# Mixture-of-experts kernel: routing ahead of the weight splits, and a first expert loop that waits for its weights expert by expert

## The reference

```python
def ffn(x):                                    # 8 experts, 2 chosen
    logits = x @ W_gate + b_gate               # W_gate [512, 8]
    _, top_idx = top_k(logits, 2)
    y_all = relu(einsum('bsd,edh->bseh', x, W_e) + b_e)   # W_e [8, 512, 512]
    return take_along_axis(y_all, top_idx[..., None], 2).mean(2)

x = x + 0.5 * ffn(layernorm(x))
x = x + attention(layernorm(x))                # one head, width 128
x = x + 0.5 * ffn(layernorm(x))                # the same weights again
```

## Time and profile before

| | us |
|---|---|
| median of 3 runs | 309.33 (308.43 to 310.49) |
| span of the profiled execution | 309.0 |
| PE busy | 258.0 (84%) |
| DVE busy | 180.9 (59%) |
| POOL busy | 147.6 (48%) |
| ACT busy | 98.5 (32%) |

### The profile page before, as it was taken

How to read it: one execution, slowest core, us unless ns; L and a number is a source line. 1 busy time by engine, 2 the same in 40 slices (tenths; PEclk the granted TensorE clock), 3 DMA queues, 4 the chain that set the end, 5 groups by cost and what they waited for, 6 DMA issues and landing times. The chain is left out here.

```text
span 309.0 us, 4801 instructions
## 1 busy us (share of the span) xinstructions
PE 258.0 (84%) x1271; PEld 184.7 (60%) x1272; DVE 180.9 (59%) x379; ACT 98.5 (32%) x177; POOL 147.6 (48%) x150
## 2 busy tenths in 40 slices
PE   7948674899999999994999998838999999999400
PEld 2314222378888888853878684413888888888300
DVE  4995989733444434367688837884344344443691
ACT  0652642324233342411234533221232433324100
POOL 4570653735666656334856400005356666563450
PEclk9975855799999999997999999996999999999955
DMA  6995641384453434526230101213354444345792
GB/s 243 378 405 200 225 137 48 97 267 158 158 169 126 148 127 161 178 68 185 78 136 0 70 15 55 83 55 97 105 147 151 167 132 159 116 159 200 286 319 108
DMA packets 22434, 47.24 MB, mean 153 GB/s; under 512 B 4237, under 2 KB 4877, under 8 KB 22417
## 3 DMA queue, kind: packets, MB, share of 16 engines
q1 hardware_dynamic: 12208, 22.35, 20.9%
q0 software_dynamic: 7360, 20.46, 20.8%
q10 hardware_dynamic: 2850, 4.23, 3.7%
HBM read 32.34 MB, written 18.35 MB: 164 GB/s over the span
## 5 line engine op out<-in xcount | busy, mean ns | idle before, releaser
L442 POOL DMA_INDIRECT z_dram<-yrow,place x46 | 46.8, 1017 | 58.3 <-ACT yrow L568 50.0
L1093 DVE TENSOR_TENSOR xt_lo<-tp_ps,xt_hi 128x512 fp32r<-128x512 f32 x46 | 31.8, 692 | 57.7 <-ACT xt_hi L561 57.1
L434 POOL DMA_INDIRECT xg<-xn_dram,tok x46 | 46.5, 1010 | 32.3 <-DVE tok L1080 17.5
L568 ACT ACTIVATE yrow<-ypre 128x512 f32<-128x512 f32 x46 | 29.1, 633 | 99.0 <-issue 50.6
L561 ACT ACTIVATE xt_hi<-tp_ps 128x512 fp32r<-128x512 f32 x46 | 26.8, 582 | 11.9 <-PE tp_ps L741 11.9
L741 PE MATMUL tp_ps<-ident,xg 128*128 128x128 f32 x184 | 27.9, 274 | 1.5 <-DMA xg<-xn_dram,tok 0.8
L427 POOL TENSOR_TENSOR rstd<-var_eps,neg_half 128x2 f32<-128x2 f32 x12 | 9.4, 787 | 40.6 <-DVE var_eps L946 38.4
L1101 DVE TENSOR_TENSOR ypre<-y_ps,be_bc 128x512 f32<-128x512 f32 x24 | 16.6, 692 | 20.8 <-PE y_ps L756 20.8
L756 PE MATMUL y_ps<-whi,xt_hi 128*128 x96 | 27.9, 413 | 0.6 <-issue 0.6
L741 PEld LDWEIGHTS tp_ps<-ident,xg 128*128 128x128 f32 x184 | 22.7, 141 | 9.1 <-issue 1.8
L694 PE MATMUL g_ps<-xt_gate,wg 128*8 128x256 f32 x64 | 20.2, 472 | 9.2 <-DVE topi L968 9.0
(11 more groups left out here) (135 smaller groups left out, 407.9 us busy)
## 6 DMA issues: line engine op xcount, KB each, us to landing
raw<-in_L_ffn_W_e_dram SPq DMA_DIRECT2D x16, 512.0 KB, 6.8
z_rows<-z_dram SPq DMA_DIRECT2D x8, 512.0 KB, 3.6
xn_dram<-xn ACTq DMA_DIRECT2D x12, 256.0 KB, 2.2
x<-in_L_attn_x_dram SPq DMA_DIRECT2D x4, 512.0 KB, 5.5
z_last<-z_dram SPq DMA_DIRECT2D x4, 512.0 KB, 6.1
out_dram<-x SPq DMA_DIRECT2D x8, 256.0 KB, 3.8
xn_dram<-xn_more ACTq DMA_DIRECT2D x4, 256.0 KB, 3.5
z_rows<-z_dram SPq DMA_DIRECT2D x4, 256.0 KB, 2.8
```

Of the source, the lines that this page charges most:

```text
L434: pool.indirect_dma_start(out=xg[:, t % XG, :], out_offset=None, in_=xn_dram[f][:, :], in_offset=bass.IndirectOffsetOnAxis(ap=tok[:, t:t + ...
L442: pool.indirect_dma_start(out=z_dram[f][:, :], out_offset=bass.IndirectOffsetOnAxis(ap=place[:, t:t + 1], axis=0), in_=yrow[:, t % YB, :], ...
L568: act.activation(yrow[:, t % YB, :], ypre[:, t % 2, :], ACT.Relu, scale=HALF_MEAN).then_inc(yrow_made, 1)
L1093: dve.tensor_tensor(xt_lo[:, t % 2, :], tp_ps[(n0 + t) % 2][:], xt_hi[:, t % 2, :].bitcast(F32), ALU.subtract).then_inc(xt_made, 1)
```

## The change

- x is loaded tile by tile (8 transfers); weight loads wait for no split. SP's queue is: x, halves 0 to 7, the stores of the normalised rows of the first layer, halves 8 to 15, and the biases of all experts as one transfer spread over 128 partitions (2.1 MB written). TensorE no longer spreads the biases.
- In the first layer ACT normalises (x * rstd + off, with off = -mean * rstd from DVE).
- Gate logits come token by token: the transposed tile is the stationary side, the gate weights move (8 columns), and a fifth matmul adds the gate bias. The copy of the logits by ACT and their transposes are gone, in both layers. The first layer has a PSUM bank for each batch's logits.
- `ones` holds 1/128, so ranks come out as tile and fraction. Ranks and one-hot rows of batches 0 to 2 are made in one go, those of batch 3 behind the marks; a one-hot row is now an operation of its own for each of the 16 columns.
- POOL splits nothing. ACT makes six high halves ahead of the marks, four behind them and the last six in the first six tiles of the expert stage. DVE makes three low halves ahead of the expert stage and thirteen in its first seven tiles.
- TensorE waits in each of the first eight products for the halves of as many experts (tile t can hold no expert above t). The first layer has eight tiles ahead of its loop, the second two as before. The six warm-up matmuls before the first product are gone, and 10 instead of 14 stand behind the first list.

```diff
@@ sync @@
+            for i in range(NT):
+                sp.dma_start(x[:, i, :], x_rows[i * P:(i + 1) * P, :]).then_inc(x_in_sem[i], 16)
+            for n in range(E):
+                load_half(n)
+            for i in range(NT):
+                sp.wait_ge(xn_made, i + 1)
+                sp.dma_start(xn_dram[0][i * P:(i + 1) * P, :], xn_at(i)).then_inc(xn_stored[i], 16)
+            for n in range(E, 2 * E):
+                load_half(n)
+            sp.dma_start(be_bc[:], b_e.rearrange("e h -> (e h)").partition_broadcast(P)).then_inc(be_in, 16)
@@ scalar @@
+            def normalise(i):
+                act.wait_ge(off_made, i // TB + 1)
+                act.activation(xn_at(i), x[:, i, :], ACT.Identity, bias=off[:, i:i + 1],
+                               scale=rstd[:, i:i + 1]).then_inc(xn_made, 1)
...
+                hi_left = list(range(HI_AHEAD, 2 * E)) if f == 0 else []
                 hi_rows(0, n0 + 1, None)
-                for t in range(HEAD + STEP):
+                for t in range(head + first * STEP):
+                    if hi_left:
+                        split_hi(hi_left.pop(0))
                     tile(t)
...
+            his = list(range(HI_AHEAD))
+            for i in range(TB):
+                normalise(i)
             for b in range(B):
+                for i in range(TB * (b + 1), min(TB * (b + 2), NT)):
+                    normalise(i)
+                for i in range(TB * b, TB * (b + 1)):
+                    copy_gate(0, i)
+                if b:
+                    split_hi(his.pop(0))
+            while len(his) > 4:
+                split_hi(his.pop(0))
+            mark_partition(0)
+            for n in his:
                 split_hi(n)
@@ tensor @@
                 for c in range(NC):
-                    last = pe.matmul(gate_ps, wg[:, c, :], xt_gate[:, c, :],
-                                     start=(c == 0), stop=(c == NC - 1))
-                last.then_inc(gate_done, 1)
+                    pe.matmul(logits(f, b)[:, i % TB, :], xt_gate[:, c, (i % TB) * P:(i % TB + 1) * P],
+                              wg[:, c, :], start=(c == 0), stop=False)
+                pe.matmul(logits(f, b)[:, i % TB, :], ones_row[:], bg[:], start=False, stop=True
+                          ).then_inc(gate_done, 1)
...
+                    if f == 0 and t < E:
+                        pe.wait_ge(hi_made, 2 * (t + 1))
+                        pe.wait_ge(lo_made, 2 * (t + 1))
...
+            for i in range(NT):
+                transpose_tile("g0", i)
+                if i == 1:
                     pe.wait_ge(gate_in, 32)
+                if i:
+                    gate(0, i - 1)
+                if i >= 4 and i % TB == 0:
+                    count(0, i // TB - 2)
+            gate(0, NT - 1)
+            count(0, B - 2)
             count(0, B - 1)
@@ vector @@
+            def row_hots(b0, b1):
+                for j in range(JB * b0, JB * b1):
+                    last = dve.tensor_scalar(row_hot[:, j, :], iota_r[:], slot_r[:, j:j + 1], None, ALU.is_equal)
+                    if j % JB == JB - 1:
+                        last.then_inc(row_hot_made, 1)
...
+                halves = list(range(LO_AHEAD, 2 * E)) if f == 0 else []
                 def tile(t):
                     if t + 1 < NS:
                         lo_rows(t + 1, n0 + t + 2)
+                    while halves and halves[0] < 2 * (t + 2):
+                        split_lo(dve, halves.pop(0), lo_made)
                     bias(t, t, f * NS + t + 1, f * NS + t - 1 if f or t >= 2 else None)
                 dve.wait_ge(eid_made, f + 1)
                 lo_rows(0, n0 + 1)
+                if f == 0:
+                    dve.wait_ge(be_in, 16)
...
+            choose(0, 0)
+            choose(0, 1)
+            split_lo(dve, 0, lo_made)
+            choose(0, 2)
+            rank_rows(0, 0, B - 1)
+            row_hots(0, B - 1)
+            split_lo(dve, 1, lo_made)
+            choose(0, B - 1)
+            route(0)
+            for n in range(2, LO_AHEAD):
+                split_lo(dve, n, lo_made)
             experts(0)
```

More of the change, by code:

```diff
@@ L190, in macaron_kernel @@
         ATT_LOADS = 5
-        x_in_sem = [sem(f"x_loaded{b}") for b in range(B)]
+        x_in_sem = [sem(f"x_loaded{i}") for i in range(NT)]
         gate_in = sem("gate_weights_loaded")
@@ L284, in macaron_kernel, with logits @@
         SUM_END = [3, 5, 7]
-        MARK_AT = 13
-        WARM = [14, 10]
-        WARM_SPLIT = 6
+        WARM = [10, 10]
         WARM_ATT = 14
[L291 to L297, removed]
+        LO_AHEAD = 3
+        HI_AHEAD = 10
+        def logits(f, b):
+            bank = g_ps if f else logit_bank[b]
+            return bank[:, 0:TB * E].rearrange("p (t e) -> p t e", e=E)
         def half(w, n):
@@ L321, in _, with load_half @@
         def _(sp):
[L322 to L328, removed]
+            def load_half(n):
                 rows = w_e[n // 2].rearrange("(c p) h -> p c h", p=P)
@@ L647, in _ @@
                 if b:
-                    copy_gate(1, b - 1)
-            copy_logits(1, B - 2)
-            copy_gate(1, B - 1)
-            copy_logits(1, B - 1)
+                    for i in range(TB * (b - 1), TB * b):
+                        store_xn(i)
+                        copy_gate(1, i)
+            for i in range(TB * (B - 1), NT):
+                store_xn(i)
+                copy_gate(1, i)
             mark_partition(1)
@@ L790, in experts @@
                                 r * STEP + (f * NS + t - 1))
-                for t in range(REST, NS):
+                for t in range(REST[f], NS):
                     tile(t)
@@ L884, in _ @@
                 if b >= 2:
-                    gate(1, b - 2)
+                    for i in range(TB * (b - 2), TB * (b - 1)):
+                        gate(1, i)
                 if b + 1 < B:
                     project_qk(b + 1)
-                if b >= 2:
-                    transpose_logits(1, b - 2)
                 transpose_prob(b)
@@ L898, in _ @@
                     count(1, b - 2)
-            gate(1, B - 2)
-            transpose_logits(1, B - 2)
+            for i in range(TB * (B - 2), TB * (B - 1)):
+                gate(1, i)
             warm_up(3, v_ps)
-            transpose_xn("g1", B - 1)
-            count(1, B - 2)
-            gate(1, B - 1)
-            transpose_logits(1, B - 1)
+            for i in range(TB * (B - 1), NT):
+                transpose_tile("g1", i)
+                if i % TB == 0:
+                    count(1, B - 2)
+                else:
+                    gate(1, i - 1)
+            gate(1, NT - 1)
             count(1, B - 1)
@@ L947, in moments, with offsets @@
                                   ALU.add).then_inc(var_made, 1)
+            def offsets(b):
+                s = TB * b
+                dve.wait_ge(rstd_made, b + 1)
+                dve.scalar_tensor_tensor(out=off[:, s:s + TB], in0=mv[:, s:s + TB, 0], scalar=-1.0,
+                                         in1=rstd[:, s:s + TB], op0=ALU.mult, op1=ALU.mult
+                                         ).then_inc(off_made, 1)
             def normalise(kind, b):
```

321 lines of the change are left out of this document (107 added, 214 removed).

## The result

The changed kernel takes 326.81 us (median, 325.63 to 327.45), the kernel before 309.61 beside it; the ratio is 1.054, with a 95% interval from 1.050 to 1.058. It is slower by 17 us where 5 us faster were forecast. The profiled execution has a span of 325.7 us, 16.7 more than the one before.

The account below looks back on a forecast made before the run. Bound by TensorE's expert products from 62.33 us, before that by routing queued behind weight splits; -4.1 (first layer) - 1.6 (attention) + 0.3 (second routing) = -5.4, giving 303.9 us; range 296 to 313.

Parts of the forecast that it names:

- part 1: First layer, routing goes first: last gate product at 22 us, `tok` at 33.6 against 54.5, first product at 41.5.
- the sum had 26: First layer's gate: at half clock throughout, TensorE has 17.6 us of work after 8.3, ending near 26.
- the second rival: Late transfers: biases arrive at 48 us, the ring starts 5.5 us later; 309.4 us, no change; chance 0.18.
- Part 2, the ring: First eight expert tiles: DVE and ACT queues wait on each other, 5.8 us a turn against 3.2 of TensorE.
- The 2.6 us for the clock: First expert tiles: allowance for TensorE losing full clock at times, taken between nothing and 5 us.
- the 21 us in front: First layer: `tok` 21 us earlier, of which 14 are given back in the first eight tiles.
- Part 3: Second layer's gate and routing: attention stage -1.6 us (0 to -2.5), tail to the list +0.3 (-1 to +1.5).
- The port rival: First expert tiles: POOL's descriptor writing holds DVE's splits, 2.0 us more a turn; 316 us, slower; chance 0.10.
- the rule that I set beside it: SBUF ports shared by DVE and POOL go to whichever starts first, so a gather can hold a split; no size.
- The sign that the prediction named for it: First layer's gate, sign of a wrong forecast: `tok` after 38, against 33.6 expected, with TensorE busy at half clock throughout.

Follow-up runs that it names:

- the gate runs: Changed kernel with the gate product of before: in both layers 314.45 us, ratio 1.015; in the second layer alone 320.93 us, ratio 1.036.
- the run with the high split moved: Changed kernel with ACT's high split of each of the first six tiles moved between xt_hi and relu: 323.33 us, ratio 1.043.
- the open ring: Changed kernel with DVE's low splits behind each tile's bias, one tile further ahead, and ACT's high split between xt_hi and relu: 317.13 us, ratio 1.020.
- both edits: Changed kernel with the gate product of before in both layers and the queue order of the open ring: 303.78 us, ratio 0.980.
- the last run: Run with both edits, plus DVE's routing order changed (second low split behind `tok`, ranks and one-hots in two goes): 297.74 us, ratio 0.963.

## Why the prediction was wrong

**The step that failed** is in part 1: "four weight loads of 128x128 and a fifth of one row, which I bound by 0.5 us ... and 1.2 us", together with "The timeline shows the fast transposes from 16 us on the earlier trace rows, so I take 22" for the last gate product. It ended at 35.2, 13.2 us later. Two errors lie in it.
- The price, the larger one: at half clock throughout the sum had 26, so 9.2 us are missing without any choice of the clock, 7.0 of them by the distance of the eight tiles. I took the row of four transposes. A gate tile is four f32 products and the bias, and the trace has each such product as two matmul records: the gate tile shows x8 + x2 records, 0.95 to 1.06 us and 0.38 at full clock, 1.71 and 0.59 at half clock; with their overlap 1.2 and 2.2 us. The tiles stand 3.07 us apart in the trace (16.9 to 20.0), where the sum had 2.2. A nearer row of before was another f32 product with 128x128 weights (line 813, the value projection), not shown ahead of the prediction:

```profile
157.21 1.95 PE L813 MATMUL v_ps<-wqkv,xt_att 128*128 128x128 f32 x16
```

  Eight such records take 1.0 us at full clock, so some 2.0 at half; as an estimate that moves the end at half clock from 26 to 32.
- The clock, the other 4 us (22 instead of 26). I took the full clock over from the trace of before, where it did not even last. The fast transposes at 16 us are followed by these rows:

```profile
24.34 3.57 PE L694 MATMUL g_ps<-xt_gate,wg 128*8 128x256 f32 x8 [5.35 <-DVE topi L968]
...
28.15 1.95 PE L681 MATMUL tp_ps<-ident,xn_more 128*128 128x128 f32 x8
```

  Both are at half clock again, behind 5.35 us of idle time, and the slices of the earlier trace rows that read 5 say the same. With the changed form of the gate product the trace shows half clock until 58 us without any idle time between 11.6 and 35 us. By the gate runs the clock in the first layer follows from this form: all three traces with the old form and the changed kernel's other edits have the full clock from 15 to 17 us to 31 or later, all five with the new form have half clock there.

With the gate product of before, `tok` still came at 39.1 instead of 33.6: the form accounts for 8.5 of the 14.0 us. The rest lies ahead of the last logits too: they were there at 27.6 and not at 22, and from them to `tok` it took 11.5. And even then the kernel took 314 us, 1.5% more than before, since `tok` comes 15.4 us earlier and the first eight products take 15.7 longer.

**The rest of part 1.** From the last gate product to `tok` I had 11.6 us, it took 12.3. The twelve one-hots took 2.04 (I took 1.4 between 1.1 and 2.2). The biases were expected at 42; their transfer, issued at 26.8, took 16.1 us to land, 42.9. DVE did not wait for them, so the second rival decided nothing.

**Part 2, the ring**, was right, and the size of a turn too: 5.69 us against 5.8. The run with the high split moved and the one with the open ring confirm its terms. That the whole stage fits as well (41.5 us against 42.0) has some luck in it: from the end of product 0 to the end of product 7 it took 36.7 us, the sum without any allowance for the clock had 36.6. The 2.6 us for the clock were meant for these turns and for tile 8. What did cost was product 0, at half clock: 4.7 us instead of 2.8. The forecast knew that this edit gives back 14 to 17 us; it stood and fell with the 21 us in front, which were 7.

**Part 3** had the wrong sign for the same reason as part 1. Attention -1.6 was +2.7 and the tail +0.3 was +3.6, together 7.6 us of the miss. Two tiles cost 2.5 us at full clock, more than the 1.89 + 0.29 that they replace, and the clock falls behind them in a stage that had it at full. 3.7 of these 6.3 us came back with the old gate in the second layer.

**The rivals.** The port rival (splits held by POOL, "316 us, slower than before") ended nearest to the time and had the wrong mechanism: every low split of the changed kernel, beside POOL's work or not, took 1.21 or 1.22 us. Of the rule that I set beside it, one half is borne out and the other is not. The Trainium skill, SBUF — State Buffer, "SBUF: two separate sides", gives the shared ports to whichever starts first, if GpSimd's operation reads SBUF. The gathers that began just behind a split took 2.0 us instead of 1.0, as it says. But splits that began inside a scatter or just behind the start of a gather were not held (61.34 and 62.47 us in the run with the high split moved); there the measurement decides. None of my rivals was about the gate, the one edit whose operation no row showed. The sign that the prediction named for it ("a `tok` after 38 with TensorE busy at half clock throughout") is what the trace shows.

What stays open: why 2.7 us are lost behind product 8 in the open ring (1.8 with both edits, nothing in the last run), and the 1.1 us of the last stretch. Nothing was run for them.

## What to carry to other kernels

Before you turn a matmul round so that the narrow side moves, count the weight loads and passes that it then has, take their price from a product of the same type and shape and not from a transpose, and don't take over the clock of a stage whose products change form: look how long it lasts in the rows of before, and give both clocks a price. When work is moved into a pipelined stage, write the order of each queue beside the others and look for a ring: the same splits cost 5.7 us a tile ahead of the bias and 3.5 behind it. And a gain in front of a stage must be compared with what the stage gives back before either is believed.

## What the hardware showed that I had not expected

In these traces a TensorE that works without a gap can have the lower clock. With the token-by-token gate product it was at work in every microsecond from 16 to 26, at half clock (four transposes 1.11 us; 0.50 where the clock was recorded); with the old gate product it was busy 8.26 of 10 us, at full clock (0.6). In the attention stage it kept the full clock at 46.7 of 49 us busy and lost it at times at 49.8 of 51. The clock also fell from full to half with no gap on TensorE just before: at 188.5 us in the changed kernel and at 196.8 us in the run with the high split moved, behind one pair of gate tiles and in the second tile of another. The Trainium skill, TensorE: Matmul & The Clock Gate, "Part 1: The HAM clock gate (the "warmup" mystery)", says that the clock gate is set by how busy the engine has been recently. By that rule these stretches would have run at full clock; the measurements decide against it, if busy is read as the profile's busy share.

The granted clock of a page reads 1.00 until its first recorded change, in these traces also where all durations are those of half clock. Two runs with the same routing in the first layer show it: the changed kernel reads 1.00 in 16 to 26 us and the run with the high split moved 0.50, with the same transposes of 1.11 us. The duration of one known operation (four transposes: 0.6 or 1.1 us) is the safer reading of the first microseconds.
